# Output stores issued by the sync engine, in between the adjacency loads, in place of ScalarE

## What is computed

```python
h = x @ W                                   # 8192 x 256
s1 = h @ attn[:256, 0];  s2 = h @ attn[256:, 0]
e = leaky_relu(s1[:, None] + s2[None, :], 0.2)
e = where(adj > 0, e, -9e15)                # adj: 8192 x 8192 int32, sparse, 268 MB
h_prime = softmax(e, axis=1) @ h
out = layernorm(x + elu(h_prime))           # 8192 x 256 float32
```

## Time and profile before

| | |
|---|---|
| median of 3 runs | 933.06 us (930.17 to 943.01) |
| profiled execution, its own time | 937.33 us |
| its span, first to last instruction | 935.1 us |
| busy in the span | PE 61%, DVE 65%, ACT 61%, POOL 66% |
| moved by DMA | 332.76 MB, mean 356 GB/s |
| queue q1 (issued by SP) | 281.29 MB |
| queue q10 (issued by ACT) | 20.98 MB |
| queue q0 (issued by POOL) | 29.79 MB |

### The profile page before, as it was taken

The page is one execution under the profiler, slowest core; times in us unless marked ns, Lnnn a source line. Parts: engine busy times, 40 slices in busy tenths (PEclk is TensorE's granted clock), DMA queues, the critical chain, the costliest instruction groups (busy, mean ns, idle before and its releaser), DMA issues. The chain is left out here.

```text
span 935.1 us, 10111 instructions
## 1 busy us (share of the span) xinstructions
PE 571.5 (61%) x2385; PEld 343.5 (37%) x2385; DVE 610.4 (65%) x2337; ACT 573.9 (61%) x531; POOL 613.9 (66%) x694
## 2 busy tenths in 40 slices
PE   5688984566475763747676376583863747477540
PEld 4566642233242432424434143341531424244320
DVE  4356543577576865669886594984865668485861
ACT  3045455659295783967786478693883949597310
POOL 4577237778757576377847877888577675577740
PEclk9799997878787978789887798887988889799875
DMA  8999979999889999799899799997999889899205
GB/s 329 393 416 418 379 293 408 418 410 397 345 343 382 408 393 402 295 387 399 359 411 400 291 422 397 383 391 288 414 414 376 313 333 392 326 394 420 69 23 202
DMA packets 65295, 332.76 MB, mean 356 GB/s; under 512 B 19558, under 2 KB 38215, under 8 KB 48720
## 3 DMA queue, kind: packets, MB, share of 16 engines
q1 hardware_dynamic: 27616, 281.29, 73.8%
q0 software_dynamic: 25456, 29.79, 10.1%
q10 hardware_dynamic: 12160, 20.98, 6.0%
HBM read 357.37 MB, written 17.14 MB: 400 GB/s over the span
## 5 line engine op out<-in xcount | busy, mean ns | idle before, releaser
L1449 POOL DMA_INDIRECT GATH<-haug,ids x448 | 477.0, 1065 | 131.2 <-issue 127.9
L1258 ACT ACTIVATE WORK<-ADJ 128x4096 bf16<-128x4096 int32 x128 | 461.4, 3606 | 93.5 <-PE pk L508 75.9
L508 PE MATMUL pk<-WORK,D 128*128 128x512 bf16 x1024 | 285.2, 430 | 242.4 <-ACT WORK L1258 242.1
L508 PEld LDWEIGHTS pk<-WORK,D 128*128 128x128 bf16 x1024 | 102.3, 107 | 409.3 <-ACT WORK L1258 287.4
L519 PE MATMUL acc<-GATH,diag 128*128 128x256 f32 x512 | 138.4, 418 | 60.7 <-DVE diag L797 60.5
L519 PEld LDWEIGHTS acc<-GATH,diag 128*128 128x128 f32 x512 | 103.2, 207 | 93.5 <-DVE diag L797 76.1
L1306 ACT ACTIVATE WORK<-WORK,smalls 128x1024 f32<-128x1024 int32 x16 | 18.4, 1148 | 153.6 <-DMA WORK<-in_adj_dram,smalls 78.1
L494 PE MATMUL acc<-Waug,GATH 128*128 128x258 f32 x256 | 64.5, 395 | 12.5 <-DVE GATH L724 12.5
L807 DVE SCALAR_TENSOR_TENSOR PART<-GATH,smalls,PART 128x256 f32<-128x256 f32 x128 | 62.2, 486 | 4.6
L776 DVE TENSOR_SCALAR smalls<-GATH,S 128x7 f32<-128x7 f32 x64 | 16.8, 263 | 65.1 <-DMA GATH<-haug,ids 65.0
L570 PE MATMUL mid_acc<-X,WORK 128*128 128x256 f32 x256 | 59.2, 385 | 0.0
(11 more groups left out here) (177 smaller groups left out, 715.0 us busy)
## 6 DMA issues: line engine op xcount, KB each, us to landing
ADJ<-in_adj_dram SPq DMA_DIRECT2D x128, 2048.0 KB, 10.7
haug<-GATH POOLq DMA_DIRECT2D x32, 258.0 KB, 8.3
WORK<-s_row ACTq DMA_DIRECT2D x16, 512.0 KB, 12.0
out_dram<-Y ACTq DMA_DIRECT2D x32, 256.0 KB, 14.7
GATH<-haug,ids POOLq DMA_INDIRECT x448
X<-in_x_dram SPq DMA_DIRECT2D x1, 4096.0 KB, 32.8
WORK<-in_adj_dram ACTq DMA_DIRECT2D x8, 512.0 KB, 17.3
WORK<-s_row SPq DMA_DIRECT2D x1, 4096.0 KB, 14.2
```

The costliest lines, as they stand in the source:

```text
L508: done = nc.tensor.matmul(pk[s % PKS][:], D16[:, k, :], A16[:, q % 2, k * BW:(k + 1) * BW], start=(half == 0 and k == 0), stop=(half == 1 ...
L1258: act.activation(A16[:, q % 2, :], ADJ[:, q % 4, :], ACT.Relu, scale=HALF_SCALE if q % 2 else 1.0, accum_out=degree[:, q // 2, q % 2:q % 2 ...
L1449: pool.indirect_dma_start(out=GATH[:, r, k * DA:(k + 1) * DA], out_offset=None, in_=haug, in_offset=bass.IndirectOffsetOnAxis(ap=ids[:, t ...
```

## The change

`store(j)` goes from ACT's queue to SP's. On SP it stands behind `load_half(q)` with `q = 2 * (pair_step(j) + 4) + 4`, the half that waits for the first count of the store's step; the next one is the half that waits for the second count. The stores whose `q` is 128 or more (four, `j` 28 to 31) come after the last load and ahead of the wait for `mid_stored` and of the 4 MB load of scores. The transfer itself, its waits and its semaphore are the same.

```diff
@@ sync engine
+            def store(j):
+                sp.wait_ge(normed, 2 * (j + 1))
+                sp.dma_start(out_tiles[:, GROUP * j:GROUP * (j + 1), :], Y[:, j % 2, :, :])\
+                    .then_inc(out_stored[j % 2], 16)
+
             for q in range(4, HALVES):
                 load_half(q)
+                for j in range(G):
+                    if 2 * (pair_step(j) + 4) + 4 == q:
+                        store(j)
+            for j in range(G):
+                if 2 * (pair_step(j) + 4) + 4 >= HALVES:
+                    store(j)
@@ scalar engine
-            def store(j):
-                act.wait_ge(normed, 2 * (j + 1))
-                act.dma_start(out_tiles[:, GROUP * j:GROUP * (j + 1), :], Y[:, j % 2, :, :])\
-                    .then_inc(out_stored[j % 2], 16)
-
...
                 for j in pairs_at(s - 2):
                     elu_exp(j)
-                for j in pairs_at(s - 4):
-                    store(j)
                 mid_pieces(s)
```

## The result

The changed kernel takes 886.12 us in the median of 4 runs (884.08 to 888.37) against 933.07 before. The ratio is 0.948, with a 95% interval of 0.942 to 0.954. I had forecast 912, with a range from 898 to 932. The profiled execution went from 937.33 to 888.37, that is 49.0 us less.

A forecast was written before the change was run, and what follows sets the result against it. It took ACT's own queue, held by the latency of transfers sharing DMA engines with 2 MB loads, as the bound. Gains of 31 less costs of 2 + 5 + 3 gave -21: profiled 916.3, median 912 us, range 898 to 932.

The forecast's parts named there:

- The store ahead of chunk loads: On ACT's ring, stores delay the loads of chunks 2 and 5 (gain 15 us) and chunk 7 (gain 2).
- ACT's wait for `normed`: ACT waits 17.5 us for `normed` ahead of stores; a third booked as gain, 6 us.
- Waits for the landing of a store: ACT waits 8.0 us in `elu_exp` for stores to land; earlier landing from SP's ring gains 5 us.
- DVE's waits for scores: DVE waits 13.4 us for scores at chunks 9 and 12, behind stores, making ACT late; gain 3 us.
- SP's waits: SP waits for `normed` with a half's load behind it, so some loads go late; cost 2 us.
- the squeeze: In the stage, a faster ACT presses the same bytes into less time, so chunk loads land later; cost 5 us.
- rival (b): In the stage, engines push one another, so the gain multiplies until transfers bound: -40, 893 us; chance 0.11.
- The tail: At the end, the 4 MB load of scores goes behind the last store and ends last; cost 3 us.
- (a): Only ring delay is gained: -10, 923 us, chance 0.22; sign: ACT's waits for PE at the count grow.
- (c): A transfer's queue doesn't matter; more halves in flight slowed chunks 2 and 5: -3, 930 us; chance 0.10.
- (d): Late half loads starve the DMA engines: 946 us, chance 0.07; sign: ACT waits over 20 us for ADJ mid-kernel.

The follow-up runs named there:

- e1: Kernel before, with ACT issuing each store one step later, ahead of that step's exponentials: median 936.01 us, ratio 1.003.
- e2: Kernel before, with ACT issuing each store behind the two chunk loads instead of ahead of them: median 931.84 us, ratio 0.996.
- e10: Kernel before, stores on ACT, with SP also issuing 28 unneeded 256 KB copies in 1 KB pieces: median 906.31 us, ratio 0.973.
- e3: Changed kernel, with ACT keeping its wait for `normed` at the old place without issuing anything: median 886.07 us, ratio 0.947.
- e5: Changed kernel, with SP issuing each store two halves later: median 917.48 us, ratio 0.981.
- e4: Kernel before, stores on ACT, with SP also waiting for `normed` where the changed kernel issues its stores: median 937.23 us, ratio 1.004.
- e6: Kernel before, with SP issuing the 4 MB load of scores only after the last store has landed: median 931.05 us, ratio 1.001.
- e7: Kernel before, stores on ACT, with each half loaded by four transfers in 4 KB pieces instead of 16 KB: median 898.58 us, ratio 0.961.
- e12: Changed kernel run again without any edit, as the base of its group on that chip: median 885.45 us, ratio 0.950.

## Why the prediction was off

**The store ahead of chunk loads (booked 15 + 2).** This is the step that failed: the right place, the right sign, and less than half the size. I took the 17.5 us of a chunk without a store as the floor, so 8.5 and 6.6 us for chunks 2 and 5. Measured are 26.0 - 9.1 = 16.9 and 24.1 - 11.7 = 12.4. With the store only taken away from ahead (e1, e2) chunk 2 landed after 15.4 and 15.7 us, chunk 5 after 14.5 and 13.8. So this alone gave about 10 us at each, and the small pieces on SP's ring some 6 and 2 to 3 more. That 17.5 was no floor stood in the trace of before: chunks 0, 1 and 7 landed after 12.6, 14.0 and 15.2 us, and the last of them has a store just ahead. At chunks 0 to 7 ACT waits 43 us less instead of the 15 to 17 booked, at 8 to 15 another 6.5 less. I had cited the rule of turns from the Trainium skill ("DMA: Bandwidth & Descriptors", "Queues, rings and completion order") for the store on ACT's ring, and did not apply it to the same store on SP's. If a turn is one piece, its 16 small pieces for each DMA engine (256 / 16, an estimate) are 16 cheap turns for the 16 pieces of a chunk's two loads; the landing of 9.1 us and e10 agree. The rule speaks of packets, which it gives as holding several pieces. The counts above would look much the same with several pieces to a turn on either ring, and can't tell that apart.

How much of the 42.9 us ahead of the last `normalise` is due to this: in e10, where only cheap turns were added and 2% more bytes, the last `normalise` ended at 884.34 + 0.42 = 884.8, 31.6 us before that of the kernel before. (These are profiled executions, and the one of before was some 4 us above its median; the medians give e10 25.5 us of gain, and the change 47.) The rest, 11.3 us, is what the clean ring of ACT adds, less the copy's own traffic. These two were not told apart.

**ACT's wait for `normed` (6).** Measured nothing (e3, where the wait is 7.1 us). I had taken a third of the 17.5 us in the table. That ACT would only have stood at a chunk or at PE instead is likely, and not shown.

**Waits for the landing of a store (5).** Measured nothing: 8.0 us before, 9.7 after. The stores land after 12.2 us in the median instead of 14.7, but the pace is higher too. e5 shows how near to the edge this is: with two more halves ahead of a store, 91.1 us.

**DVE's waits for scores (3).** The 13.4 us are gone. All scores land after 7.5 to 11.9 us, those of chunk 9 after 8.3 instead of 23.5. In e1 and e2 they are gone too, and the time stayed, with new waits for stores in their place. What they were worth alone was not tried.

**SP's waits (cost 2) and the squeeze (cost 5).** For the first, e4 measures 0 to 0.7%, with its own stores on ACT and a third of the waits (28.4 against 86.2 us up to 780); at the changed kernel's pace it was not measured. For the second there are 29 us more of waiting for halves. What they took back was not measured either, but the total gain was not eaten. I had said that the 409 GB/s of the best 60 us left 55 us, and then didn't believe in more than 31. The ceiling was not the error: the stage now averages 400 GB/s, below 409, though it holds 412 for 300 us. The time came near rival (b)'s number (893), with transfers as the bound. Its mechanism, engines that push one another, isn't needed to explain the gain, and was not tested.

**The tail (cost 3).** Wrong in sign: -6.0 us. I followed the 4 MB load and not what came after the last store. The chain ended at 927.4 in a span of 935.1, and I never asked for the 7.4 us between. They follow POOL's last wait, which is for the last store, and that store was slow because it shared with the load (10.96 us against 2.12 in e6, where the load comes behind it). Now it lands after 2.2 us, and no closing time shows behind the load, which took 11.8 us instead of the 14.2 I used. e6 got 4.1 of the 6.0 us with this alone.

Of the rivals, (a) and (c) are out by the size. (a)'s sign didn't come either: ACT's waits for PE at the count are 74.7 us, 75.9 before. (c) is out also by e1 and e2, where chunks 2 and 5 without a store ahead land after 14 to 16 us, and by e10. (d) is out by the result, though its sign came.

## What to carry to other kernels

When a small transfer and a stream share the DMA engines, the small one's latency is roughly its time alone plus, for each of its pieces on a DMA engine, the time of one piece of the stream. An estimate for the store, with 16 pieces for each engine: a 16 KB piece of SP's took 0.70 us (chunk 4 before, 398 pieces on 16 engines in 17.5 us), a 4 KB piece 0.23 (chunk 4 in e7, 532 in 7.6 us). That gives 2.1 + 11.3 = 13.4 and 2.1 + 3.7 = 5.8 us, where 14.7 and 7.9 were measured. Look for the small transfer that an engine waits for, and then either cut the stream into smaller pieces (e7: 3.9% here) or put what is not urgent and made of small pieces on the stream's own ring. There it queues behind the stream, and its buffer comes free later: two halves more cost 31 us (e5). Before moving a transfer, ask also what it does to the others from its new place, and what in the end stage begins only when it has landed.

## What the runs showed of the hardware

- Adding traffic can make a kernel faster: 28 copies of 256 KB in pieces of 1 KB on SP's ring took the kernel from 931.8 to 906.3 us (e10).
- With halves in pieces of 16, 8 and 4 KB, ACT waits 94.3 (e12), 40.4 and 12.9 us at the chunks in the changed kernel, and the time is 885, 888 and 892 us. With the DMA engines at some 400 GB/s, a shorter latency bought nothing here.
- A 256 KB store lands after 2.1 to 2.3 us when alone, after 14.7 beside 16 KB pieces on another ring, and after 7.9 beside 4 KB pieces.
